# Segment sums in a seven-pass graph kernel: one scan over 16 or 17 features in place of one for each feature

## The reference, cut to what matters

```python
messages = x[src] * edge_probs[:, None] * weight                 # pass 0
out = jax.ops.segment_sum(messages, dst, num_segments=N_NODES)
m = jnp.einsum('ei,eio->eo', hx[edge_src], W)                    # passes 1 and 2
agg = jax.ops.segment_sum(m, edge_dst, num_segments=n_nodes)
p = jnp.exp(e - m[dst])                                          # passes 3 and 4 (3 heads, 1 head)
out = jax.ops.segment_sum(h[src] * alpha[:, :, None], dst, num_segments=N)
s = jax.ops.segment_sum(x_src * mask[:, None], dst, num_segments=x.shape[0])   # passes 5 and 6
```

## Time and profile before

| what | value |
| --- | --- |
| median of 3 runs | 24749.61 us (24730.12 to 24751.8) |
| profiled execution, its own time | 24703.6 us |
| its span in the profile | 24702.3 us |
| mean granted TensorE clock | 0.883 of full speed |
| busy: PE, DVE, ACT, POOL | 80%, 58%, 5%, 74% |

### The profile page before, as it was taken

One profiled execution on the slowest core, in us unless ns is written; L12 is line 12 of the kernel. 1 busy time (PEld: TensorE's weight loads), 2 busy tenths in 40 slices (PEclk: granted clock), 3 DMA queues, 4 the chain that ended last, 5 costly groups with the idle time before them and its releaser, 6 DMA issues.

```text
span 24702.3 us, 328868 instructions
## 1 busy us (share of the span) xinstructions
PE 19828.3 (80%) x124988; PEld 13345.9 (54%) x124988; DVE 14221.7 (58%) x31398; ACT 1123.5 (5%) x2172; POOL 18400.7 (74%) x18458
## 2 busy tenths in 40 slices
PE   6688778888788888766767477777689999988885
PEld 6688744444444454455555333333378887544443
DVE  6577667777667777656666534333356666333333
ACT  0000000000000000100000000000010000000000
POOL 7777777777777777777777677777757777677776
PEclk9899889999889999888888688888789999799997
DMA  5344422222122222133333222222233333222221
GB/s 155 99 131 132 118 51 54 54 54 54 41 54 54 54 54 54 37 90 99 100 102 102 59 67 72 70 71 72 63 97 112 112 113 106 53 58 59 59 58 42
DMA packets 1190681, 1902.10 MB, mean 77 GB/s; under 512 B 398267, under 2 KB 766709, under 8 KB 1180669
## 3 DMA queue, kind: packets, MB, share of 16 engines
q1 hardware_dynamic: 596752, 1670.28, 20.0%
q0 software_dynamic: 590528, 209.38, 8.6%
q10 hardware_dynamic: 1837, 1.39, 0.0%
HBM read 1258.97 MB, written 620.63 MB: 76 GB/s over the span
## 4 chain that ended last, share of the span: by engine, by line
POOL 72%; issue 22%; PE 3%; DVE 1%; DMA 0%; SPq 0%; ACT 0%; DVEq 0%; ACTq 0%; POOLq 0%
POOL gb L516 70%; PE psB L811 1%; POOL ext L531 1%; POOL ext L506 1%; PE psA L800 1%; SPq L338 0%; PE psB L829 0%; PE psB L834 0%; DVE Sb L1104 0%; PE psB L687 0%; DVE prod L1139 0%; PE psA L823 0%; DVE prod L1429 0%; DVE prod L1424 0%; ACT prod L584 0%
## 5 line engine op out<-in xcount | busy, mean ns | idle before, releaser
L687 PE MATMUL psB<-xp,arena 128*128 128x224 bf16 x58170 | 6007.3, 264 | 688.1 <-DVE arena L1007 620.0
L687 PEld LDWEIGHTS psB<-xp,arena 128*128 128x128 bf16 x58170 | 5701.0, 100 | 1443.3 <-issue 820.6
L687 PE MATMUL psB<-ext,arena 128*128 128x280 bf16 (+1 forms) x20874 | 3376.7, 325 | 1238.0 <-DMA arena<-oh_d 1223.6
L749 PE MATMUL psB<-w2as,hid 128*128 128x512 f32 x6448 | 3298.3, 643 | 845.3 <-DVE prod L1139 845.3
L687 PEld LDWEIGHTS psB<-ext,arena 128*128 128x128 bf16 x20874 | 2092.5, 101 | 2488.1 <-DMA arena<-oh_d 1253.6
L516 POOL DMA_INDIRECT gb<-tab2b,srci x2604 | 2720.4, 1045 | 793.6 <-issue 793.6
L516 POOL DMA_INDIRECT gb<-tab1b,srci x2728 | 2636.2, 966 | 848.8 <-issue 831.1
L516 POOL DMA_INDIRECT gb<-tab1a,srci x2728 | 2633.7, 965 | 842.8 <-issue 831.1
L516 POOL DMA_INDIRECT gb<-tab3b,typi x2604 | 2492.8, 957 | 913.7 <-issue 793.3
L516 POOL DMA_INDIRECT gb<-tab2a,srci x2356 | 2610.3, 1108 | 718.2 <-issue 718.2
L1139 DVE TENSOR_TENSOR prod<-psB,gb 128x1024 f32<-128x1024 f32 x1612 | 1974.1, 1225 | 1829.0 <-PE psB L749 953.1
(11 more groups left out here) (315 smaller groups left out, 15979.8 us busy)
## 6 DMA issues: line engine op xcount, KB each, us to landing
arena<-oh_d SPq DMA_DIRECT2D x1324, 448.0 KB
oh_d<-arena SPq DMA_DIRECT2D x558, 448.0 KB
hid<-oh_d SPq DMA_DIRECT2D x515, 448.0 KB
ext<-oh_d SPq DMA_DIRECT2D x207, 448.0 KB
S2a<-Sb SPq DMA_DIRECT2D x62, 1404.0 KB
S2b<-Sb SPq DMA_DIRECT2D x62, 884.0 KB
S3a<-Sb SPq DMA_DIRECT2D x62, 832.0 KB
gb<-tab1a,srci POOLq DMA_INDIRECT x2728
```

The lines of the kernel that those rows point to most:

```text
L687: m = pe.matmul(psB[b][:, u * 512:u * 512 + W], pk.onehot(n)[:, g, u * P:(u + 1) * P], pk.part(g, i), start=g == 0 and i == 0, stop=g == N ...
L749: m = pe.matmul(psB[g % 2][:, i * 512:(i + 1) * 512], hid[:, o:o + P], w2as[:, :], start=True, stop=True)
```

## The change

Four things change.

- The messages of a chunk lie in `prod` feature by feature (`run`): 52 edges of feature 0, then 52 of feature 1, and so on. The message products therefore read `gb` with a stride and write without one.
- One scan runs over 16 or 17 features at once (832 or 884 elements), in place in `prod`. Its decay is a tile `kept` that holds the 52 decays 16 or 17 times over, with 0 at the first edge of each feature. The carry over the chunk's border is added to the first edge of every feature by one small VectorE instruction (two in passes 3 and 4).
- ScalarE fills `kept` (`decay_row`, `decay_heads`) and copies the sums from feature order to the edge order of `Sb` (`turn_state`). The store of a chunk and the fix of a pass wait for that copy (`a_state`) and no longer for the scan.
- `OFF[3]` is 16 and no longer 14: pass 3 gathers 36 columns of each chunk and picks 8 pairs. The store's place among SP's one-hot loads is now a table, `SLOT`: ahead of all the chunk's loads in passes 0, 1, 2, 5 and 6.

```diff
-OFF = (18, 8, 8, 14, 10, 16, 10)
+OFF = (18, 8, 8, 16, 10, 16, 10)
+SLOT = (0, 0, 0, 0.65, 0.55, 0, 0)
+REPS = (1, 1, 1, 3, 1, 1, 1)
...
-                sp.wait_ge(d_sum, NCH * k + c + 1)
+                sp.wait_ge(a_state, NCH * k + c + 1)
                 sp.dma_start(rows(Sd[k], fwidth[k])[:, span(c), :], state(c, fwidth[k])).then_inc(l_out[c % 2], 16)
...
-                    done = onehots_until(pk, done, pk.until(c, 0.9 * (fwidth[k] - 1) / fwidth[k]))
+                    done = onehots_until(pk, done, pk.until(c, SLOT[k]))
                     put(k, c)
...
+            def decay_row(k, c):
+                if c < 2:
+                    a.wait_ge(d_rep, k + 1)
+                else:
+                    a.wait_ge(d_sum, NCH * k + c - 1)
+                a.activation(v3(kept(k, c), TC)[:, :, 1:TC], bc(same[:, c * TC + 1:(c + 1) * TC], 1, 16), ACT.Copy).then_inc(a_rep, 1)
+
+            def turn_state(k, c):
+                f = fwidth[k]
+                n, base = (f - (3 if k == 3 else 1), 0) if k in (3, 4) else (f, 2048 if k in (1, 2) else 0)
+                a.wait_ge(d_sum, NCH * k + c + 1)
+                if c >= 2:
+                    a.wait_ge(l_out[c % 2], 16 * (31 * k + c // 2))
+                a.activation(state(c, f)[:, :, f - n:f], run(n, base).rearrange("p f t -> p t f"), ACT.Copy).then_inc(a_state, 1)
+                if k not in (3, 4) and c + 2 < NCH:
+                    decay_row(k, c + 2)
...
-            def sums(k, c, width, done, cols, data, decay):
-                pk, f = PICK[k], fwidth[k]
-                now, old = state(c, f), state(c + 1, f)
-                share = pk.share(c, done)
-                stored(k, c)
-                v.drain()
-                for i, q in enumerate(cols):
-                    done = picks(k, done, pk.until(c, share + (0.9 - share) * i / len(cols)), width)
-                    m = v.tensor_tensor_scan(now[:, :, q], decay(q), data(q), old[:, TC - 1, q:q + 1] if c else 0.0, ALU.mult, ALU.add)
+            def sums(k, c, base=0):
+                f = fwidth[k]
+                data, old = run(f, base), state(c + 1, f)
+                v.drain()
+                if c:
+                    v.scalar_tensor_tensor(data[:, :, 0], old[:, TC - 1, :], same[:, c * TC:c * TC + 1], data[:, :, 0], ALU.mult, ALU.add)
+                v.wait_ge(a_rep, NCH * sum(REPS[:k]) + c + 1)
+                v.drain()
+                for q in range(0, f, 16):
+                    n = min(16, f - q)
+                    d = prod[:, base + q * TC:base + (q + n) * TC]
+                    m = v.tensor_tensor_scan(d, kept(k, c)[:, 0:n * TC], d, 0.0, ALU.mult, ALU.add)
                 m.then_inc(d_sum, 1)
...
-                        m = v.tensor_tensor(pr[:, :, h * w + 1:(h + 1) * w], gv[:, :, 0:D], bc(p3[:, :, h], 2, D), ALU.mult)
+                        m = v.tensor_tensor(data[:, h * w + 1:(h + 1) * w, :], gv[:, :, 0:D].rearrange("p t f -> p f t"),
+                                            bc(p3[:, :, h], 1, D), ALU.mult)
...
+                    for i, (q, n) in enumerate(((0, 17), (17, 17), (34, 17)) if k == 3 else ((0, 17), (17, 16))):
+                        if i:
+                            done = picks(k, done, pk.until(c, 0.45 + 0.1 * i), width)
+                        at = prod[:, q * TC:(q + n) * TC]
+                        if k == 3 or i == 0:
+                            v.wait_ge(a_rep, NCH * (3 if k == 3 else 6) + (3 * c + i if k == 3 else c) + 1)
+                        m = v.tensor_tensor_scan(at, kept(k, i if k == 3 else 0)[:, 0:n * TC], at, 0.0, ALU.mult, ALU.add)
...
-                    v.tensor_tensor(pr, got(c, width), bc(wE[:, span(c)], 2, width), ALU.mult).then_inc(d_gbfree, 1)
-                    v.drain()
-                    done = sums(k, c, width, done, range(width), lambda q: pr[:, :, q], lambda q: same[:, span(c)])
+                    v.tensor_tensor(run(width), got(c, width).rearrange("p t f -> p f t"), bc(wE[:, span(c)], 1, width), ALU.mult
+                                    ).then_inc(d_gbfree, 1)
+                    sums(k, c)
                     done = picks(k, done, pk.until(c, 1), width)
```

More of the change, by code:

```diff
@@ L243, in gnn_program @@
             sem(f"d_{n}") for n in ("first", "zero", "key16", "find", "count", "cum", "ends"))
-        d_code, d_keep, d_row, d_typed, d_gbfree, d_sum, d_product, d_xe, d_zz = (
-            sem(f"d_{n}") for n in ("code", "keep", "row", "typed", "gbfree", "sum", "product", "xe", "zz"))
+        d_code, d_keep, d_row, d_typed, d_gbfree, d_sum, d_product, d_xe, d_zz, d_rep, d_decay, d_head = (
+            sem(f"d_{n}") for n in ("code", "keep", "row", "typed", "gbfree", "sum", "product", "xe", "zz", "rep", "decay", "head"))
         d_fix, d_fixexp, d_fixrow, d_input, d_evac, d_mid, d_act, d_block, d_stage, d_nodes = (
@@ L316, in state, with kept, run, decays @@
             return v3(Sb[:, o:o + TC * f], f)
+        def kept(k, c):
+            if k in (3, 4):
+                return (xT16 if c % 2 == 0 else xT32)[:, 0:17 * TC]
+            o = (c % 2) * TC * 56 + TC * 40
+            return Sb[:, o:o + TC * 16]
+        def run(F, base=0):
+            return prod[:, base:base + F * TC].rearrange("p (f t) -> p f t", t=TC)
+        def decays(k):
+            H = 3 if k == 3 else 1
+            return v3(sub[:, TC * H:2 * TC * H], H)
         def last_state(k):
@@ L611, in hidden_units @@
                     a.activation(hid[:, (h % 2) * 512:(h % 2 + 1) * 512], psA[h % 2][:, :], ACT.Relu, bias=b1s[:, 0:1]).then_inc(a_hid, 1)
+                for c in range(turned_to, NCH):
+                    turn_state(k, c)
             def exp_edges(k):
@@ L618, in exp_edges @@
                     a.activation(da, da, ACT.Exp).then_inc(a_exp, 1)
+                    decay_heads(k, c)
+                    turn_state(k, c)
             def typed_rows(pk):
+                turned_to = 0
                 for m in range(pk.last):
+                    if m == pk.pairs * (turned_to + 1) + 2:
+                        turn_state(pk.k, turned_to)
+                        turned_to += 1
                     a.wait_ge(t_turn, pk.typed0 + m + 1)
@@ L626, in typed_rows @@
                     a.activation(pk.xT[0:pk.F, o:o + 2 * P], psA[0][0:pk.F, 0:2 * P], ACT.Copy).then_inc(a_row, 1)
+                for c in range(turned_to, NCH):
+                    turn_state(pk.k, c)
             for k in range(7):
+                if k not in (3, 4):
+                    decay_row(k, 0)
+                    decay_row(k, 1)
+                if k == 0:
+                    for c in range(NCH):
+                        turn_state(k, c)
                 if k in (1, 2):
@@ L1157, in softmax_pass @@
                 exs = [v3(arena[:, (2 + i) * TC * 12:(2 + i) * TC * 12 + TC * ef], ef) for i in range(2)]
-                pr = v3(prod[:, 0:TC * H * w], H * w)
+                data = run(H * w)
+                clear_decays(k)
                 done = picks(k, 0, pk.until(-1, 1), width)
@@ L1167, in softmax_pass @@
                     stored(k, c)
+                    turned(k, c)
                     v.drain()
```

68 lines of the change are left out of this document (50 added, 18 removed).

## The result

| what | before | after |
| --- | --- | --- |
| median | 24748.1 us | 24900.71 us |
| lowest to highest | 24730.12 to 24751.8 | 24884.96 to 24919.8 |
| profiled execution, its own time | 24703.6 us | 24919.8 us |

The change makes the kernel slower by 0.64%: the ratio of after to before is 1.0064 [1.0052, 1.0077], or 153 us between the medians.

The account below looks back on a forecast made before the run. Gathers on POOL bound the kernel, held by instructions with two SBUF inputs. Summed, -155 + 208 + 46 - 28 + 86 + 25 + 82 = +264 us on 24703.6 gave 24,970 us predicted, range 24,650 to 25,250.

Parts of the forecast that it names:

- Fewer gathers: Pass 3 on POOL: 124 gathers fewer at 1.249 us each, -155 us, covered by picking an eighth pair a chunk.
- Scans of 1.93 and 2.05 us: VectorE's long scans: 832 elements were to take 1.93 us and 884 elements 2.05, at 2.16 ns an element.
- Products of 1.55 and 3.0 us with L994's surcharge: Message products reading gb strided: 832 elements 1.02 + 0.53 = 1.55 us, 1664 elements 1.90 + 1.1 = 3.0 us.
- I take the middle: Two long scans in a row (passes 0, 4, 5): the hold priced midway between held through (+370 us everywhere) and let go (+158).
- Pass 3, -28 us: Holds of pass 3's gathers by products, three separate scans and other pieces: 5.75 us a chunk against 6.2, -28 us.
- Passes 1 and 2: Holds by one long scan a chunk in these passes: 1.1 us against 0.9, +25 us for both.
- pass 6: Holds there: product 0.75 us and scan 1.15 a chunk, against 0.6 before, +82 us.
- let-go parts: The sum if paired long scans let a gather go between them everywhere: +158 us.
- At nothing: ScalarE's fills and copies priced at zero: turn_state 2.5 us for 1664 elements, 4 for 2652; pass ends 0 to +10 us.
- The products keep their old price: Rival: strided message products get no longer, -226 us on the forecast, 24,740 us; chance 20%.
- A long scan doesn't hold: Rival: gathers pass during long scans, so the scans' shares, 880 us, fall away, 24,090 us; chance 7%.
- TensorE and VectorE pace pass 5: Rival: these engines, not POOL's gathers, set pass 5; with a late one-hot load +161 us, 25,130 us; chance 13%.

Follow-up runs that it names:

- e1: The kernel before with only OFF[3] raised from 14 to 16 (two more picked columns a chunk in pass 3): 24546.76 us, 0.9917 of before.
- e3: The changed kernel with the repeated decays of passes 0, 3 and 4 in PSUM, scans of 8 or 9 features: 24529.94 us, 0.9910 of before.
- e4: The changed kernel with a one-element copy in place of each long scan of pass 5: 24818.66 us, 1.0027 of before.
- e5: The kernel before (short scans) with OFF[3] = 16 and the decays of passes 3 and 4 in PSUM: 24109.87 us, 0.9738 of before.
- e6: e5 plus pass 0's decays and the message products' weights of passes 0, 3 and 4 in PSUM: 23950.22 us, 0.9672 of before.
- e7: The changed kernel with scans of 4 features, not 16, in passes 0, 1, 2, 5 and 6: 24703.13 us, 0.9976 of before.

## Why the prediction was right, point by point

The sign, the engine and the mechanism were right: slower, on POOL, because instructions with two SBUF inputs hold gathers that start in them. The size was too large: +264 us against +153 between the medians, or +164 in the profiles without the 52 us of a slower base. The forecast of 24,970 us is 69 us above the measured median.

- **Fewer gathers, -155 us: right.** e1 has this part alone, -176 in the profiles of which 23 are holds.
- **Scans of 1.93 and 2.05 us: right**, 1.89 and 2.00.
- **Products of 1.55 and 3.0 us with L994's surcharge: right** in passes 0, 4, 5 and 6 (1.55, 3.14, 3.04, 1.55). In pass 3 it was too low, 1.85 us. There the weights of the three heads are interleaved too, so two inputs are read with a stride; that this is the reason was not tested.
- **"I take the middle": the step that was mis-sized.** For two long scans in a row the prediction had a bound held through and one let go between them. The trace of after shows them always let go: in passes 4 and 5 the pairs caught 122 gathers each, and none waited past the end of the scan in which it began. With that bound the sum had been +158, stated beside +264, and the parts come out as well: pass 5 169 us (found 164, or 158 without the 3 ns of base), pass 4 7 (found 4, or -4), pass 0 57 (found 68, or 61). The hints were in the rows. In the earlier trace rows a gather is let go between two products. And the earlier trace rows was read wrongly: the gather at 12020.22 does not slip by. It begins in the fourth scan of the run, which ends at 12020.41, and ends 0.82 us after that, at 12021.23. So it was caught and let go at the first border; only the later one was held to the end of the run. Half the weight went to a rule, that a caught gather waits until the whole run ends, which the same rows contradict.
- **Pass 3, -28 us: found 0.** Two errors that partly cancel, which is luck. The products held 135 us where 88 were predicted, being 0.3 us longer each; the three scans held 218 in place of 251. The rest of the pass held 33 in place of 19, about 7 of it the base. Why the scans held less is not known.
- **Passes 1 and 2 too high, pass 6 right.** +25 were predicted and +29 found, but 16 of these are the 3 ns of base, so the scans cost 13. For pass 6 +82 were predicted and +88 found, 80 without the base.
- **Its arithmetic** has two slips. The let-go parts add up to +157, not +158. And the second scan of a pair let go costs 0.69 us by the prediction's own formula (1.93 - 1.24) where it has 0.6; in the let-go sum that is about 5 us each in passes 4 and 5.
- **At nothing: right in effect, wrong in size.** `turn_state` takes 3.6 us for 1664 elements and 5.7 for 2652, not 2.5 and 4. The copy reads with a stride, which L618 doesn't; that this is the reason was not tested. ScalarE has room for it all the same, 2996 us busy of 24,918. At the passes' ends 0 to +10 us were predicted, 11 came.

The rivals. **The products keep their old price** is ruled out by the products' rows. **A long scan doesn't hold** is ruled out too: e3 and e4 take 60 to 212 us out of the passes in which they free or remove the long scans. The inference of the Trainium skill (SBUF — State Buffer, Who interferes with whom) that descriptor generation needs the write interface, so that a two-input product would stall no indirect DMA, does not hold here: the gather beside the product of pass 5 takes 3.04 us in place of 0.944. Another rule of that section, that an instruction with at most one SBUF input outside the two-port modes doesn't contend with GpSimd, agrees with e5 and e6. **TensorE and VectorE pace pass 5**: its sign is there, since VectorE's wait for tab3a shrank from 226 us to 38. But POOL never waits for a buffer in the pass, and the gathers that were held by the product (139 us) and by the scans (98 us) account for 237 of its 240 us. The cover became thin and was not used up; in e7, with 48 us fewer holds in the pass, it is.

## What to carry to other kernels

When the chain goes through an engine that issues indirect DMAs, count what the other engines do to it: work on an idle VectorE is not free if both its inputs lie in SBUF. Such an instruction of 1.5 us or more costs the bottleneck about its length less 0.8 us, and nearly all of any length that is added to it, whatever the change saves on VectorE. Moving one small repeated operand (a decay, a weight) to PSUM gave about 2.4% on top of e1 (e1 to e6; 3.3% with the two picked columns), where the change as a whole cost 0.6%. Then look at what is next: in e7 one pass had already passed from POOL to VectorE and TensorE. And where a sum hangs on one behaviour with two outcomes, don't average them: take the rows at hand apart, instruction by instruction, and look for a case of each.

## What the runs showed of the hardware that had not been expected

- **A gather caught early in a run of short scans is let go at the next border, one caught late mostly isn't.** Scans of 832, 884 and 208 elements let a waiting gather go at the first border between two of them. So do the first scans of a run of 52-element ones. The trace of before has 936 gathers that a run of short scans delayed with a border still ahead, each counted by the scan that runs 0.12 us after its start. Of the 519 in one of the first six scans of their run, 507 were let go at the next border. Of the 417 caught later, 31 were; 298 waited for the end of the run and 88 for some border between. The earlier trace rows has one of each kind, in the fourth and in the tenth scan. e1 repeats it: 516 of 524, and 27 of 436. In no run was a gather caught by a long scan in seventh place or later with a border ahead (e7 has them up to the fifth scan). Almost all gathers caught late are also the second or third that meet their run. So what decides, the place in the run, its earlier gathers or the length of the scans, stays open.
- **One operand in PSUM frees the gathers**, at the same speed of the scan: 52 elements take 0.306 us with the decays in PSUM (e5) and 0.313 in SBUF (e1), and the products of pass 3 take 1.02 us either way (e6, before).
- **A strided write costs more than a strided read** in a two-input product: 832 elements take 1.02 us plain, 1.55 with the gathered rows read with a stride, and 1.85 written with one; 1664 take 1.90, 3.04 and 3.6.
- **The median gather moved between executions**, from 944 to 947 ns, worth 52 us. Why is not known; it sets how finely two single profiles can be compared.
- Not tried: decays in PSUM for passes 1, 2, 5 and 6, where TensorE writes the same PSUM tiles in the course of the pass. The table of e6 bounds what such an edit could still give: at most 76 + 75 + 82 + 37 us, and in passes 5 and 6 most of the holds are at the products.
